# The rotated half of the queries: products on the matrix engine, or DMAs within SBUF

## What is computed

```python
q = rms_norm(hidden_states @ wq_a, q_a_norm_w) @ wq_b
q = q.reshape(b, s, NH, Q_HEAD).transpose(0, 2, 1, 3)      # NH = 16, Q_HEAD = 64 + 64
q_nope, q_pe = (q[..., :QK_NOPE], q[..., QK_NOPE:])
def rotate_half(x):
    x1, x2 = jnp.split(x, 2, axis=-1)
    return jnp.concatenate([-x2, x1], axis=-1)
def apply_rope(x, cos, sin):
    x = x.reshape(b, h, s, d // 2, 2).transpose(0, 1, 2, 4, 3).reshape(b, h, s, d)
    return x * cos + rotate_half(x) * sin
q_pe = apply_rope(q_pe, cos, sin)
attn = jnp.einsum('bhqd,bhkd->bhqk', query_states, key_states) * SOFTMAX_SCALE
attn = softmax(attn);  out = jnp.einsum('bhqk,bhkd->bhqd', attn, value_states)
```

## Time and profile before

| | us |
|---|---|
| median of 3 runs | 1098.09 |
| the profiled execution | 1111.73 |
| its span, first to last instruction | 1109.5 |
| PE busy | 1022.8 |
| DVE busy | 726.3 |
| ACT busy | 524.6 |
| POOL busy | 473.3 |
| the 32 pairs, about | 320 to 805 of the span |

### The profile page before, as it was taken

One profiled execution on the slowest core, in us unless ns is written; L12 is line 12 of the kernel. 1 busy time (PEld: TensorE's weight loads), 2 busy tenths in 40 slices (PEclk: granted clock), 3 DMA queues, 4 the chain that ended last, 5 costly groups with the idle time before them and its releaser, 6 DMA issues.

```text
span 1109.5 us, 22666 instructions
## 1 busy us (share of the span) xinstructions
PE 1022.8 (92%) x6232; PEld 808.0 (73%) x6233; DVE 726.3 (65%) x1649; ACT 524.6 (47%) x1139; POOL 473.3 (43%) x417
## 2 busy tenths in 40 slices
PE   4548999999879999999999999999999879999995
PEld 4436888888557777777777777777688648888884
DVE  6344566664377778878887788777546746656542
ACT  1224343332156677676767677666501313533321
POOL 2541343443344454646355654443225513344432
PEclk9999999999998999999999999999999989999998
DMA  9833455433200110111111011111476545644330
GB/s 241 274 111 96 106 140 125 109 51 49 63 1 10 58 39 26 33 40 39 39 39 30 30 39 39 39 39 39 154 227 210 185 134 110 163 107 104 53 57 8
DMA packets 71615, 95.87 MB, mean 86 GB/s; under 512 B 9616, under 2 KB 48656, under 8 KB 71312
## 3 DMA queue, kind: packets, MB, share of 16 engines
q1 hardware_dynamic: 56656, 77.51, 22.8%
q0 software_dynamic: 14304, 16.87, 9.1%
q10 hardware_dynamic: 576, 0.53, 0.2%
HBM read 64.37 MB, written 34.43 MB: 89 GB/s over the span
## 4 chain that ended last, share of the span: by engine, by line
PE 53%; DMA 26%; issue 9%; DVE 7%; POOLq 1%; ACT 1%; another core or an unknown queue 1%; POOL 1%; SPq 0%; DVEq 0%; ACTq 0%
DMA x_after_moe<-shared,small 13%; DMA out<-shared,small 12%; PE bank L1720 11%; PE bank L1747 10%; PE bank L1708 5%; PE bank L1709 5%; PE bank L1710 5%; PE bank L1819 3%; PE bank L1695 2%; PE bank L1696 2%; PE bank L1521 1%; PE bank L1523 1%; PE bank L1525 1%; PE bank L1662 1%
## 5 line engine op out<-in xcount | busy, mean ns | idle before, releaser
L874 ACT ACTIVATE shared<-bank,small 128x512 f32<-128x512 f32 x256 | 176.7, 690 | 93.0 <-DVE small L1334 92.1
L1334 DVE TENSOR_REDUCE small<-bank 128x1 f32<-128x512 f32 x256 | 174.9, 686 | 43.7 <-PE bank L1710 43.4
L1720 PE MATMUL bank<-constants,shared 128*128 128x128 f32 x1024 | 157.0, 276 | 2.1 <-ACT shared L883 1.1
L810 ACT CAST split_rows_and_inner<-bank 128x512 fp32r<-128x512 f32 x78 | 45.8, 588 | 238.5 <-PE bank L1506 199.4
L1720 PEld LDWEIGHTS bank<-constants,shared 128*128 128x128 f32 x1024 | 123.1, 141 | 44.7 <-issue 14.3
L1523 PE MATMUL bank<-expert_weights_low,split_rows_and_inner 128*128 x312 | 144.2, 462 | 0.0
L1525 PE MATMUL bank<-expert_weights_high,split_rows_and_inner 128*128 x312 | 143.1, 459 | 0.0
L1521 PE MATMUL bank<-expert_weights_high,split_rows_and_inner 128*128 x312 | 125.2, 401 | 3.5 <-DVE split_rows_and_inner L1119 3.4
L1708 PE MATMUL bank<-expert_weights_high,shared_split 128*128 128x512 f32 x256 | 123.5, 483 | 3.7 <-DVE shared_split L1402 2.3
L1124 DVE TENSOR_TENSOR split_rows_and_inner<-bank,split_rows_and_inner 128x512 fp32r<-128x512 f32 x78 | 53.9, 691 | 106.1 <-ACT split_rows_and_inner L810 104.4
L573 POOL DMA_INDIRECT x_after_moe<-shared,small x39 | 61.2, 1569 | 143.2 <-DMA x_after_moe<-shared,small 90.2
(11 more groups left out here) (197 smaller groups left out, 2192.7 us busy)
## 6 DMA issues: line engine op xcount, KB each, us to landing
expert_weights<-L_ffn_w_kernel SPq DMA_DIRECT2D x32, 512.0 KB
shared<-rows_by_expert SPq DMA_DIRECT2D x78, 129.0 KB
expert_weights<-L_ffn_wo_kernel SPq DMA_DIRECT2D x16, 512.0 KB
shared<-inverse_sums SPq DMA_DIRECT2D x64, 128.0 KB, 3.0
attended_transposed<-shared SPq DMA_DIRECT2D x32, 256.0 KB, 3.1
expert_weights<-attended_transposed SPq DMA_DIRECT2D x2, 2048.0 KB, 10.1
shared<-attended_transposed SPq DMA_DIRECT2D x2, 2048.0 KB
rows_by_expert<-empty_rows SPq DMA_DIRECT2D x19, 129.0 KB
```

What stands on the lines that cost most here:

```text
L874: nc.scalar.activation(prob[k % 4], bank[k % 4][:, :], ACT.Exp, bias=negmax[:, k % 8:k % 8 + 1], accum_out=psum[par][:, hh * GT + qt:hh * ...
L1334: V.tensor_reduce(negmax[:, k % 8:k % 8 + 1], bank[k % 4][:, :], AX.X, ALU.max, negate=True).then_inc(max_ready, 1)
L1720: last = tr(bank[4 + k % 2][:, c * P:(c + 1) * P], prob[k % 4][:, c * P:(c + 1) * P], ident)
```

## The change

For the pairs from the third on, part 1 of the queries is no longer computed. After DVE has made `ropeA`, ACT copies bank 7 as it is into a new SBUF area (`unturned`, 128 x 512). SP then issues four DMAs from SBUF to SBUF, each 32 partitions by 512 columns (64 KB), which put block 1 where block 0 was, and so on, into `ropeB`. DVE's second multiplication waits for all four (`queries_turned`) and works on `ropeB` in place. [...] PE's last part waits for ACT's copy instead of for the second multiplication. POOL splits two parts of the weights instead of three, and DVE places part 1 of the weights for two pairs only, with no sign. The first two pairs still use the two products. (`add_due` and one other semaphore of POOL become one.)

```diff
-    c[:, C_SIN:C_ALL] = np.tile(sin.T, (4, 1))
+    c[:, C_SIN:C_ALL] = np.concatenate([-sin.T, sin.T, -sin.T, sin.T])
...
+        unturned = area(F32_SHARED + F32R_SHARED, [S])
...
+            def turn_queries(p):
+
+                sp.wait_ge(unturned_sb, p - 1)
+                sp.wait_ge(rope_ready, p)
+                for a in range(4):
+                    b = a + 1 - 2 * (a % 2)
+                    sp.dma_start(ropeB[a * HALF:(a + 1) * HALF], unturned[b * HALF:(b + 1) * HALF]).then_inc(turned_in, 16)
...
+            turn_queries(2)
             spread(0, 0)
+            turn_queries(3)
             spread(1, 1)
+            turn_queries(4)
             load_prep(3)
             for p in range(NPAIR - 4):
                 store(p, p % 2)
                 spread(p + 2, p % 2)
+                if p + 5 < NPAIR:
+                    turn_queries(p + 5)
...
+            def queries_unturned(p):
+                act.wait_ge(ropeA_sb, p + 1)
+                if not among(p, 2):
+                    act.wait_ge(turned_in, (p - 2) * 64)
+                nc.scalar.copy(unturned, bank[7][:, :]).then_inc(unturned_sb, 1)
...
+                    if k == (5 if first else 4) and p + 2 < NPAIR:
+                        queries_unturned(p + 2)
                     if k in BY_ACT:
                         copy_pT(p, par, k)
...
-                    dve.wait_ge(qb_psum, p + 1)
-                    V.tensor_tensor(ropeB, query_bank(p, 1)[:, :], qsin, ALU.mult).then_inc(ropeB_sb, 1)
+                    if among(p, 0, 1):
+                        dve.wait_ge(qb_psum, p + 1)
+                        turned = query_bank(p, 1)[:, :]
+                    else:
+                        dve.wait_ge(turned_in, (p - 1) * 64)
+                        turned = ropeB
+                    V.tensor_tensor(ropeB, turned, qsin, ALU.mult).then_inc(ropeB_sb, 1)
...
-                    if k == 6 and p + 2 < NPAIR:
-                        queries(p + 2, par, 1)
```

More of the change, by code:

```diff
@@ L166, in build @@
         shared_at = -(-nc.sbuf_base // 32) * 32
-        shared = sb("shared", [P, F32_SHARED + F32R_SHARED])
+        shared = sb("shared", [P, F32_SHARED + F32R_SHARED + S])
         split = nc.alloc_sbuf_tensor_at("shared_split", [P, F32R_SHARED], F32R, offset=shared_at + 4 * F32_SHARED)
@@ L321, in build @@
         tag_sb = sems("tag_sb", 2)
-        add_due = sems("add_due", 2)
+        pool_issue = sem("pool_issue")
         added = [sems(f"added{f}_", 3) for f in range(2)]
@@ L328, in build @@
         k_high, k_low, v_kept = sem("keys_high"), sem("keys_low"), sem("values_kept")
-        wc_high, wc_low_due, wcur_ready = (sem(f"query_weights_{k}") for k in ("high", "low_due", "ready"))
+        wc_high, wcur_ready = (sem(f"query_weights_{k}") for k in ("high", "ready"))
         qa_psum, qb_psum, qz_psum = sem("qa_psum"), sem("qb_psum"), sem("qz_psum")
+        unturned_sb, turned_in = sem("queries_unturned"), sem("queries_turned")
         ropeA_sb, ropeB_sb, rope_ready = sem("ropeA_sb"), sem("ropeB_sb"), sem("rope_ready")
@@ L571, in add_results @@
                         pool.wait_ge(added[f][(v - 1) % 3], (t - 1) // 3 * 16 + 16)
-                    pool.sem_inc(add_due[f], 1)
+                    pool.sem_inc(pool_issue, 1)
                     nc.gpsimd.indirect_dma_start(
@@ L590, in load_weights @@
             def load_weights(p, par):
-                src = wpair[:, p % PAIRS, :, :]
+                parts_ = slice(0, 3) if among(p, 0, 1) else slice(0, 3, 2)
+                src = wpair[:, p % PAIRS, parts_, :]
                 if p > 1:
                     pool.wait_ge(qz_psum, p - 1)
-                nc.gpsimd.tensor_copy(wch[par], src).then_inc(wc_high, 1)
+                nc.gpsimd.tensor_copy(wch[par][:, parts_, :], src).then_inc(wc_high, 1)
                 pool.wait_ge(wc_high, p + 1)
-                pool.sem_inc(wc_low_due, 1)
-                nc.gpsimd.tensor_tensor(wcl[par], src, wch[par].bitcast(F32), ALU.subtract).then_inc(wcur_ready, 1)
+                pool.sem_inc(pool_issue, 1)
+                nc.gpsimd.tensor_tensor(wcl[par][:, parts_, :], src, wch[par][:, parts_, :].bitcast(F32),
+                                        ALU.subtract).then_inc(wcur_ready, 1)
             def rope_sum(p):
@@ L1215, in _ @@
                     V.tensor_copy(wpair[:, :, 0, at + two * HALF:at + (two + 1) * HALF], src[:, :, hh, :])
-                    last = V.tensor_scalar(wpair[:, :, 1, at + (1 - two) * HALF:at + (2 - two) * HALF], src[:, :, hh, :],
-                                           -1.0 if two else 1.0, None, ALU.mult)
+                    last = V.tensor_copy(wpair[:, 0:2, 1, at + (1 - two) * HALF:at + (2 - two) * HALF], src[:, 0:2, hh, :])
             last.then_inc(wa_ready, 1)
@@ L1691, in queries @@
                         pe.wait_ge(invT_sb, p - 2)
+                elif among(p, 1):
+                    pe.wait_ge((ropeA_sb, ropeB_sb)[part - 1], p + 1)
                 elif not among(p, 0):
-                    pe.wait_ge((ropeA_sb, ropeB_sb)[part - 1], p + 1)
+                    pe.wait_ge(unturned_sb, p - 1)
                 to = query_bank(p, part)
```

## The result

The changed kernel takes 1115.43 us in the median of 4 runs (1112.82 to 1122.88), the kernel before 1100.91 us beside it (4 runs): a ratio of 1.0137, 95% interval 1.0091 to 1.0182. The forecast was +4 us.

A forecast was written before the change was run, and what follows sets the result against it. PE was taken to bound the attention. At D = 3.7 us, 20 pairs add 6.0 us, six give -0.3, three -1.4 and the first -0.5: about +4 on 1098.09, so 1102 us, range 1091 to 1122.

The forecast's parts named there:

- What bounds the kernel, and what is removed: PE sets the pace in mid-attention; 30 pairs lose two products of 0.47 us, at most 14.1 us gained.
- The cap: PE's round 0 transposes wait for ACT's copy of round 6, limiting the gain to 6.7 us at most.
- the six pairs at 0.47: Pairs where preparation keeps PE behind ACT's copies anyway, so each can gain the full 0.47 us.
- The place of the loss: DVE's multiplication waits for DMAs ahead of its round 7 copy, delaying PE's round 1; 0.3 to 0.8 us PE wait.
- the break-even: The D beyond which PE loses time in round 1: 3.45 us in the worked pair, 3.4 taken for 20 pairs.
- D: Time from ACT's copy ending to DVE's second multiplication starting: three issues, a landing, semaphores; 3.7 us, between 2.2 and 4.8.
- rows 4 to 6: Profile rows of a pair standing for 13, where ACT's copy leaves at most 0.15 us gain each.
- The likeliest case: The forecast itself: D from 3.55 to 3.98 us, costing 0 to 11 us; chance 0.38.
- rival 3: Turned halves late, D from 3.98 us: DVE stalls in round 7, 2 us or more, PE in round 1; 1117 us, chance 0.29.
- 1: DMAs in time, D up to 3.55 us; ACT's copies limit the gain to 0 to 6.7 us, about 1094; chance 0.24.
- 2: The whole 14.1 us saved on PE reach the end, 1084 us; chance 0.04.
- 4: PE's clock falls as well after stalls in 26 pairs, adding 78 us, about 1195 us; chance 0.05.

The follow-up runs named there:

- the one that lifts it: Changed kernel with sine multiplication two rounds later, cosine multiplication moved from round 4 to 7, ACT's copy awaiting the product alone; ratio 0.9926 to the kernel before.
- the first experiment: Changed kernel without any DMA, DVE's second multiplication reading ACT's copy itself, halves not exchanged; stretch of value products 453.0 us, ratio 0.9969 to the kernel before.

## Why the prediction was right or wrong

**What bounds the kernel, and what is removed.** Right: the two products take 0.47 us a pair on PE, and with no DMA at all 5.0 of 13.6 us reached the end.

**The cap.** Right in its mechanism, as the experiment without DMAs and the one that lifts it show. Of the 6.7 us at most, 6.2 fell into the measured stretch, and 5.0 came: three of the six pairs at 0.47 gave nothing, 1.4 us, as DVE's work on the keys fills them; the three with one piece of preparation more, counted at 0.15, gave 0.31 to 0.33.

**The place of the loss.** Right: DVE waits in front of the multiplication, the copy of round 7 comes late, PE waits in round 1. In seven late pairs in a row each is 0.44 to 0.51 us longer from the cosine multiplication to round 1, against 0.46 from the break-even with the D measured. The way from the multiplication to round 1 took 1.44 us for the 1.42 assumed.

**D, the term that was mis-sized.** The landing was 2.0, as taken from two rows and a straight line. The issue was taken as 0.55, "As 64 and 128 rows cost the same"; four in a row measured 0.61 each. It is mostly the place in the row that makes them longer, and the trace of before already had it: of its two broadcasts of 64 rows the first took 0.45 us and the second 0.60 in the median, which the 0.55 of 1.09 / 2 hid. The two DMAs of 64 rows within SBUF took 0.48 and 0.60, the one of 128 rows 0.49. So three issues made 1.85 us for 1.65, and D was 3.91 for 3.7. Why an issue right behind another takes longer is open. In 26 pairs, 0.21 us makes 5.5 us: this is the largest part of the 9 that were missing. The formula itself, 26 D - 92.4, gives +9.3 at 3.91, or +9.8 without the first pair, which lies ahead of the stretch.

**The classes of pairs.** The three pairs with one piece of preparation more were counted as like rows 4 to 6, and left out as slightly better. They are worse: their cosine multiplication meets an ACT that is busier, so the copy starts later, and they lost 0.71 to 0.82 each instead of 0.3, 1.4 us together. The six pairs that prepare in rounds 3 and 6 should have gained 0.05 each; they lost 0.16 to 0.23, and one of them 1.22: its four issues took 3.45 us instead of 2.44, one of them 1.6, and D was 4.90. It did so in both traces of the changed kernel (4.82 in the second). Over all 30 pairs the times from the cosine multiplication to round 1 add up to +11.3 us, or +11.8 without the first, and the stretch to +13.0. The rest stands between round 1 and the next cosine multiplication: 0.02 to 0.04 us in most pairs, 0.09 in one, and 0.14 to 0.18 ahead of the cosine multiplication of the three pairs with one piece more. What causes it is not shown.

**The range and the chances.** 1115.4 lies in the range of 1091 to 1122. The likeliest case, D from 3.55 to 3.98, held as to D in 25 of the 30 pairs, but the stretch came out over 3 us longer than my formula gives at the same D, which carried the result over the 11 us into rival 3. With ends of 2.2 and 4.8 for D and a slope of 26 us for each us, the forecast of the sign stood on 0.15 us of D: that it came true is partly luck.

**The rivals.** 1 fell (D was too long). 2 fell with the first experiment. 3 came by its size only: DVE waits 1.45 us on average, not the 2 us that were named as its sign. 4 did not come: PE waits about 0.5 us at a time for DVE's copy, and the granted clock is 1.00 from 500 to 700 us. What was called free was free: ACT's copy, the later store and POOL's later sum all stand in the kernel with the later multiplication too, whose stretch is that without any DMA.

**The bridge to the median** was wrong, and harmless. I had spread the 1.2% between the profiled execution and the median evenly over the run; most of it was one wait of 12.2 us long before the attention.

**One transfer for four, and the landing.** The Trainium skill's rule to use one transfer of all partitions instead of two to disjoint halves ("DMA: Bandwidth & Descriptors", "Rules for kernel authors") is borne out in D, 3.9 us for four, 3.1 for two and 2.4 for one. In the stretch the four cost time (471.1), while two (454.1) and one (454.2) are the same, as both D lie under the break-even. The single one here exchanged nothing, and its D was not the 2.05 of the prediction. The 2.15 us for the landing, an estimate from the fit in the Trainium skill (same page, "Anatomy of one DMA"), is near the 2.0 measured for 64 KB within SBUF. The page gives that fit for DMAs issued by GpSimd; these were issued by SP. That the D of 3.85 made with it came near 3.91 is luck: its landing is 0.15 too long and the issues beside it are 0.2 too short.

## What to carry to other kernels

When a DMA takes over an engine's product, ask first where its consumer stands in program order and what urgent work is queued behind that; moved behind it, the same DMAs cost nothing here, and in front of it they cost 18 us. Work taken from the busiest engine gives only the distance to the next chain, which the timeline shows (0.15 us of 0.47 in the commonest kind of pair); look for an operation that can leave that chain as well. And several small DMAs in a row cost their issues, here 0.6 us each on one queue, before the last of them starts; read an issue time from DMAs that stand right behind one another.

## What the runs showed of the hardware

- Within SBUF, a DMA landed 1.8 us after its issue began for 16 KB in 32 rows, 2.0 for 64 KB in 32 rows, 2.4 for 128 KB in 64 rows and 2.4 for 256 KB in 128 rows, while 128 KB broadcast from DRAM took 2.9 to 3.0.
- The issue of such a DMA on SP's queue took 0.59 us in the median for 32 rows, with 64 KB or with 16 KB, and 0.49 for 128 rows when it stood alone. By place: the first of four took 0.54 and those behind it 0.59; of two with 64 rows the first took 0.48 and the second 0.60.
- DVE's multiplication took the same 0.68 to 0.69 us with its first operand in SBUF as in PSUM.
